# A graph layer on one core: 140 sorted supers in place of 136, and GpSimd's gathers signalled from single products

## The reference

```python
def reference(x, src, dst, edge_type_16, L0_gnn_weight):
    h = jnp.maximum(_layernorm(x, axis=-1), 0.0)
    # _L0_gnn_ref(h, weight, src, dst, etypes):
    h_src = feat[src]
    for r in range(16):
        mask = etypes == r
        msg = msg + h_src * mask[:, None] @ weight[r]
    out = segment_sum(msg, dst, num_segments=6250)
    return x + out
```

## Time and profile before

| | |
|---|---|
| median of three executions | 1234.6 us |
| the profiled execution's own time | 1229.24 us |
| its span | 1227.5 us |
| mean granted clock of TensorE over the span | 0.983 |
| TensorE products (PE) busy | 1081.7 us, 88% |
| VectorE (DVE) busy | 918.1 us, 75% |
| ScalarE (ACT) busy | 437.2 us, 36% |
| GpSimd (POOL) busy | 708.6 us, 58% |
| chain that ended last, by engine | PE 70%, issue 10%, DVE 8%, ACT 5% |

### The profile page before, as it was taken

One profiled execution on the slowest core, in us unless ns is written; L12 is line 12 of the kernel. 1 busy time (PEld: TensorE's weight loads), 2 busy tenths in 40 slices (PEclk: granted clock), 3 DMA queues, 4 the chain that ended last, 5 costly groups with the idle time before them and its releaser, 6 DMA issues.

```text
span 1227.5 us, 38318 instructions
## 1 busy us (share of the span) xinstructions
PE 1081.7 (88%) x15079; PEld 724.9 (59%) x15079; DVE 918.1 (75%) x2711; ACT 437.2 (36%) x1128; POOL 708.6 (58%) x674
## 2 busy tenths in 40 slices
PE   3998998888899889899888989989988898898897
PEld 1445665565666656566565656656665665666665
DVE  7756777887777788787777777777777787777774
ACT  4784232333333333333233333333333332333332
POOL 2214666566656666666665666666666666666630
PEclk9999999999999999999999999999999999999999
DMA  6794222111122212121221112222211221212211
GB/s 171 311 393 169 58 59 60 56 49 48 58 60 59 58 49 58 50 58 58 59 58 50 54 52 58 58 60 58 59 52 46 58 57 58 59 58 58 57 35 56
DMA packets 42263, 93.40 MB, mean 76 GB/s; under 512 B 14923, under 2 KB 14925, under 8 KB 42084
## 3 DMA queue, kind: packets, MB, share of 16 engines
q1 hardware_dynamic: 13490, 40.95, 9.7%
q0 software_dynamic: 20640, 21.18, 8.4%
q10 hardware_dynamic: 7954, 28.79, 6.1%
HBM read 63.29 MB, written 27.59 MB: 74 GB/s over the span
## 4 chain that ended last, share of the span: by engine, by line
PE 70%; issue 10%; DVE 8%; ACT 5%; another core or an unknown queue 4%; DMA 3%; ACTq 0%; DVEq 0%; POOL 0%; SPq 0%; POOLq 0%
PE ps L1268 32%; PE ps L1253 19%; PE ps L1295 6%; DVE u L943 3%; ACT u L599 3%; PE ps L1310 2%; PE ps L1170 2%; DMA table<-u 2%; PE ps L1194 2%; PE ps L1161 2%; DMA w_cat<-weight 1%; DVE spreadv L855 1%; PE ps L1112 1%; PE ps L1183 1%
## 5 line engine op out<-in xcount | busy, mean ns | idle before, releaser
L526 POOL DMA_INDIRECT u<-table,row_idx x611 | 641.4, 1050 | 402.9 <-PE ps L1268 137.9
L1268 PE MATMUL ps<-u 64*64 64x512 bf16 (+1 forms) x7072 | 471.1, 378 | 35.1 <-issue 30.6
L669 ACT CAST u<-ps 128x384 bf16<-128x384 f32 (+1 forms) x612 | 256.4, 465 | 582.5 <-PE ps L1253 492.8
L943 DVE TENSOR_SCALAR u<-iota_key,z_sb 128x512 bf16<-128x512 f16 x1156 | 351.2, 368 | 112.2 <-PE ps L1268 78.1
L1268 PEld LDWEIGHTS ps<-u 64*64 64x64 bf16 x7072 | 213.1, 106 | 231.5 <-issue 110.2
L1253 PE MATMUL ps<-parts,u 128*128 128x192 bf16 x3332 | 328.3, 250 | 23.0 <-issue 21.1
L1253 PEld LDWEIGHTS ps<-parts,u 128*128 128x128 bf16 x3332 | 271.5, 99 | 57.6 <-issue 53.9
L933 DVE TENSOR_SCALAR u<-u,node_id 128x1152 bf16<-128x1152 f16 (+2 forms) x408 | 178.6, 493 | 0.0
L678 ACT COPY u<-ps 128x512 f32<-128x512 f32 x136 | 73.1, 590 | 75.0 <-remote 44.9
L963 DVE TENSOR_TENSOR accT<-accT,ps 128x32 f32 x238 | 44.7, 188 | 59.9 <-DVE accT L963 21.0
L1295 PE MATMUL ps<-u,w_cat 128*64 128x128 f32 x1088 | 78.8, 278 | 6.3 <-issue 4.7
(11 more groups left out here) (131 smaller groups left out, 643.4 us busy)
## 6 DMA issues: line engine op xcount, KB each, us to landing
u<-rel_dram SPq DMA_DIRECT2D x68, 544.0 KB
table<-u ACTq DMA_DIRECT2D x24, 1024.0 KB, 5.3
u<-table,row_idx POOLq DMA_INDIRECT x611
rel_dram<-rel_row SPq DMA_DIRECT2D x68, 4.2 KB
x_sb<-x SPq DMA_DIRECT2D x2, 448.0 KB
out<-h_sb SPq DMA_DIRECT2D x3, 224.0 KB
out<-h_sb ACTq DMA_DIRECT2D x3, 224.0 KB
msg_x<-table,spill_row POOLq DMA_INDIRECT x34
```

The lines of the kernel that those rows point to most:

```text
L526: pool.indirect_dma_start(out=msg_p[:, b, j, :], out_offset=None, in_=table, in_offset=bass.IndirectOffsetOnAxis(ap=row_idx[:, j, m:m + 1] ...
L669: act.copy(msg_s[:, u % MB, 0:width, :].rearrange("p q c -> p (q c)"), ps[gather_bank(u)][:, 0:width * ROW]).then_inc(s_gev, 1)
L943: dve.tensor_scalar(khot[:, v % KR, :], iota_key[:, :], z_sb[:, n % 3, 1, q:q + 1], None, ALU.is_equal).then_inc(s_khot, 1)
L1268: last = pe.matmul(ps[3 + a][half * D:(half + 1) * D, keys], msg_s[rows, u % MB, q % 2, part * D:(part + 1) * D], khot[rows, v % KR, keys] ...
```

## The change

NS becomes 140, so there are 70 pairs in place of 68 and 35 groups of four in place of 34; the windows of gathered edges go from 102 to 98, their tiles from 611 to 583, and all fetches, with those of the edges left over from the sort, from 645 to 618. The end of 12 supers, in place of 8, is prepared inside the loop.

GpSimd no longer waits for a count of one of eight semaphores. There is one semaphore, `s_go`, that TensorE increments once for each fetch. It does so at any of 4495 modelled spots: each product of `gather` that doesn't end a bank, the fourth product of each range in `sum_sorted`, and each product of `weigh` but the last. The planner's numbers for the pieces of the stream are altered a little, and the least distance of two spots is 1.2 in place of 0.7.

```diff
-    NS, SJ, SQ, SK, SW, GR = 136, 7, 17, 3, 32, 4
+    NS, SJ, SQ, SK, SW, GR = 140, 7, 17, 3, 32, 4
...
-        for b in banks_of(n, c):
-            now += 0.082 * SK * min(2, SQ - 2 * b)
-            marks.append((now, "gat", n * GB + b + 1))
+        for q in ranges_of(n, c):
+            for t in range(q * SK, min(q * SK + SK, NT)):
+                now += 0.082
+                if not ends_bank(q, t):
+                    spots.append(now)
...
-    FIRST, LAST, LANDED, LEAST = 0.0, now - 24.0, 5.0, 0.7
+    FIRST, LAST, LANDED, LEAST = 0.0, now - 24.0, 5.0, 1.2
...
-        mark = min((mark for mark in marks if mark[0] >= due), default=marks[-1], key=lambda mark: abs(mark[0] - at))
-        due = mark[0] + LEAST
+        go = min((s for s in range(len(spots)) if spots[s] >= due), key=lambda s: abs(spots[s] - at))
+        due = spots[go] + LEAST
...
+            def wait_for_sign():
+                begun[0] += 1
+                pool.wait_ge(s_go, begun[0])
...
+            def spot(ins):
+                if passed[0] in signs:
+                    ins.then_inc(s_go, 1)
+                passed[0] += 1
...
-                    if q % 2 == 1 or q == SQ - 1:
-                        last.then_inc(s_gat, 1)
+                        if ends_bank(q, t):
+                            last.then_inc(s_gat, 1)
+                        else:
+                            spot(last)
...
-                        sums(q, 1, 1)
+                        spot(sums(q, 1, 1))
...
+                    if r < R - 1:
+                        spot(last)
                     if r == R // 2 - 1:
-                        last.then_inc(s_mid_fl, 1)
```

More of the change, by code:

```diff
@@ L141, in gnn_program @@
     before = lambda m: m * PJ
-    marks, starts, now = [], [], 0.0
+    ends_bank = lambda q, t: t == NT - 1 or q % 2 == 1 and t == q * SK + SK - 1
+    spots, starts, now = [], [], 0.0
     for i, (n, c) in enumerate(STREAM):
@@ L146, in gnn_program @@
         now += 0.1
-        for b in banks_of(n, c):
-            now += 0.082 * SK * min(2, SQ - 2 * b)
-            marks.append((now, "gat", n * GB + b + 1))
+        for q in ranges_of(n, c):
[3 more added lines that the diff above has]
+                    spots.append(now)
+        now += 0.38 * (turned(n, c) is not None) + 0.31 * (spilled(n, c) is not None)
         if i:
             now += 0.14
[L152 to L160, removed]
+            for b in banks_of(*STREAM[i - 1]):
+                for q in range(2 * b, min(2 * b + 2, SQ)):
+                    now += 0.214
+                    spots.append(now)
+                now += 0.214 if 2 * b + 1 < SQ else 0.107
+        now += 0.5 * (c == 0 and n > 0) + 0.22 * (permuted(n, c) is not None) + 0.45 * (ranked(n, c) is not None)
         if n >= 2 and n % 2 == 0 and c == weigh_at:
-            marks += [(now + 0.95, "mid", n // 2), (now + 1.9, "fl", n // 2)]
-            now += 1.9
+            for r in range(R):
+                now += 0.13
+                if r < R - 1:
+                    spots.append(now)
     starts.append(now)
-    FIRST, LAST, LANDED, LEAST = 0.0, now - 24.0, 5.0, 0.7
-    marks.sort()
+    FIRST, LAST, LANDED, LEAST = 0.0, now - 24.0, 5.0, 1.2
     FETCHES = PALL + NGR
-    fetches, tile_time = [], []
+    spilled_fetch, tile_time, go_spots = [], [], []
     due = 0.0
@@ L176, in gnn_program @@
         at = max(at, starts[2 * four + 1]) if spills else at
-        mark = min((mark for mark in marks if mark[0] >= due), default=marks[-1], key=lambda mark: abs(mark[0] - at))
-        due = mark[0] + LEAST
-        fetches.append((mark, four if spills else None))
+        go = min((s for s in range(len(spots)) if spots[s] >= due), key=lambda s: abs(spots[s] - at))
+        due = spots[go] + LEAST
+        go_spots.append(go)
+        spilled_fetch.append(four if spills else None)
         if not spills:
-            tile_time.append(max(at, mark[0]))
+            tile_time.append(max(at, spots[go]))
     place = [min(n for n in range(NPR) if starts[n] >= tile_time[before(m) + len(tiles_of(m)) - 1] + 1.4 + LANDED or n == NPR - 1)
@@ L341, in gnn_program @@
         s_gp = [sem(f"s_gp{k}") for k in range(PRING)]
-        s_hotp, s_sump, s_mid_fl = sem("s_hotp"), sem("s_sump"), sem("s_mid_fl")
+        s_hotp, s_sump, s_go = sem("s_hotp"), sem("s_sump"), sem("s_go")
         s_over = sem("s_over")
@@ L497, in _ @@
             pool.wait_ge(s_tev, PIECES)
[L498 to L504, removed]
+            begun = [0]
+            def wait_for_sign():
+                begun[0] += 1
+                pool.wait_ge(s_go, begun[0])
             def fetch_spilled():
-                w = fetch_at_mark()
+                w = spilled_fetch[begun[0]]
                 b = w % 2
+                wait_for_sign()
                 pool.wait_ge(s_xwin, w + 1)
@@ L522, in _ @@
                 for j in tiles_of(m):
-                    while fetches[0][1] is not None:
+                    while spilled_fetch[begun[0]] is not None:
                         fetch_spilled()
-                    fetch_at_mark()
+                    wait_for_sign()
                     pool.indirect_dma_start(
@@ L529, in _ @@
                     ).then_inc(s_gp[b], 16)
-            while fetches:
+            while begun[0] < FETCHES:
                 fetch_spilled()
@@ L1233, in _ @@
                     sort_ranks(2)
+            signs, passed = set(go_spots), [0]
+            def spot(ins):
+                if passed[0] in signs:
+                    ins.then_inc(s_go, 1)
+                passed[0] += 1
             def gather(n, c):
```

## The result

The changed kernel takes 1201.0 us (median of 4, 1199.11 to 1205.48) against 1235.0 us of the kernel before beside it: ratio 0.9733, 95% interval 0.9713 to 0.9754. The forecast was 1200 us. The time is as forecast.

What follows compares the result with a forecast made beforehand. TensorE's stream was taken as the bound, with 217 us of holes following GpSimd's fetches. +23 us of work and -57 us from the spread gave -34 from 1234.6, rounded to 1200 us; 8-in-10 range 1148 to 1248.

Steps and rivals of the forecast that it cites:

- The work of two more pairs: TensorE's stream: two more pairs and 28 fewer tiles raise work from 908 to 931 us, +23 us, all on the path.
- The signals: TensorE's products: 618 semaphore increments cost nothing, at worst 6 us.
- The spread: GpSimd's fetches: coming more evenly, they cut the loss from holes in TensorE's stream from 217 to 160 us, gaining 57.
- The factor 0.77: Holes in TensorE's stream per fetch: 0.188 us in place of 0.243, applied to the whole loss.
- a tally by the distance of neighbouring fetches: TensorE's lateness per fetch in the trace: mean 0.243 us, crowded 0.455, evenly spaced 0.10.
- The shares of 60, 25 and 15%: Fetches after the change: 60% even (0.10 us of holes), 25% at today's mean (0.24), 15% crowded (0.455).
- The tally's last figure: Fetches with both preceding distances above 1.7 us: 0.02 us of holes each, in 17 cases.
- The first rival: Holes belong to TensorE's own stream and each added pair brings its own: +31 us, 1266 us; chance 0.12.
- The second: POOL is again late for every second fetch, holes go with the number of fetches: +14 us, 1249 us; chance 0.12.
- The third: The spread of fetches works nearly in full, 104 us of loss: -90 us, 1145 us; chance 0.10.
- The fourth: DVE becomes the bound as a faster TensorE asks for one-hots sooner; 945 us of DVE work; folded into the range.
- The rule that speaks against it: Skill text: engine and DMA ports are disjoint, TensorE never waits on them; by it, spreading fetches would bring nothing.

Runs made afterwards that it cites:

- idle_signs: marks140 plus the changed kernel's increments on TensorE's products, for which nobody waits; GpSimd goes by the old marks: 1198.9 us, ratio 0.9728.
- signs136: Changed kernel's signals with the old 136 supers and old least distance 0.7: 1232.5 us, ratio 1.0007 to the kernel before.
- marks140: Kernel before with 140 supers and its old marks for the fetches: 1193.2 us, ratio 0.9689.
- skip28: Kernel before (136 supers, old marks) with 28 of its 611 ordinary fetches left out, all sums kept: 1200.9 us, ratio 0.9744.
- twins: Changed kernel with every second fetch issued right behind the first, without its own signal: 1214.1 us, ratio 0.9860 to the kernel before.
- few: Changed kernel with only about 50 of 618 fetches issued, TensorE's products unchanged: 1059.7 us, ratio 0.8606 to the kernel before.
- hw_queue: few plus 544 plain DMAs of the same size issued by SyncE, on the third chip: 1050.9 us, ratio 0.9979 to the kernel before.
- signs144: Changed kernel with 144 supers, on the third chip: 1083.4 us, ratio 1.0286 to the kernel before.
- marks144: Kernel before with 144 supers and its old marks: 1165.9 us, ratio 0.9468.

## Why the prediction came out right, and where it was wrong

*The work of two more pairs, +23 us: holds.* The shortest durations of sums and gathers are alike in every kernel (2.07 us for 36 sums), and the third chip is in keeping with it: 1053 to 1100 us for 12 supers more, of which 69 would be work and 22 come back.

*The signals, nothing, at worst 6 us: within that.* idle_signs allows 6 us and signs136 nothing; the runs don't tell them apart.

*The spread, 217 to 160 us of loss: the right sum for the wrong reason.* The loss is 165 us. The factor 0.77 was built from a tally by the distance of neighbouring fetches (0.455 us where crowded, 0.10 where even), and I took the correlation for the lever. This step failed, and four runs say so: signs136, with the finer signals alone, gains nothing; marks140, without them, gains at least as much as the change; skip28, with the old signals and 28 fetches fewer, gains 31 us; twins, with a third more fetches back to back, loses 13 to 16 us, where the tally's prices asked for 75. What stands in its place is that 140 supers bring fewer fetches for each microsecond of TensorE's work, 0.71 to 0.66, which I had in the text only as 1.5 us of even distance. The spacing itself is worth what twins shows, about 0.3 us for each of the 51 fetches that twins puts closer than 1.3 us, where the tally has a difference of 0.36.

That the sum came out is luck: I scaled by number and by a factor for the spread, 0.96 x 0.77 = 0.74. The loss fell to 165 / 217 = 0.76, and marks140, without any finer signals, has 133 / 196 = 0.68 of the cost of fetches before. The shares of 60, 25 and 15% had no source either. The planners' own clocks put 155 of 644 distances under 1.25 us before, none at zero, and 89 after, but 91 with the old marks and 140 supers: they too give the wider spacing to the supers. The tally's last figure, 0.02 us with both distances above 1.7, is said to be of 17 cases; the trace has 51.

*The first rival (holes of TensorE's own)* falls with few: 141 us go when the fetches go, on a chip that has the holes. *The second (POOL stays crowded, +14)* had its mark come true and its price not: 43% of the fetches are still back to back, and the kernel got faster. *The third (in full, 1145)* did not happen, though few shows that there was that much to win. *The fourth* is not seen: DVE is at 78%, with 938 us of the 945 that I had given it.

*The rule that speaks against it*, of the Trainium skill, "SBUF — State Buffer", section "SBUF: two separate sides", says that TensorE never waits on a memory port for others. On the first two chips TensorE's stream does have holes from GpSimd's fetches: 2.58 us for 36 sums against 2.09 without. Whether a memory port is their path no run here tells, so the rule is not contradicted in what it says, but it was no guide to the time.

*What stays open* is what in a fetch holds TensorE up, and why not on the third chip. It is not rows or bytes; it grows steeply as fetches get denser. I had supply of TensorE's instructions in mind; no run tries it, and the late signals speak against it, since a product that is only issued late should still signal on time, as it does on the third chip wherever TensorE waits for another engine. Whether it is GpSimd's part of the fetch or its packets could be told by hw_queue on one of the first two chips, which was not run. Each chip was measured in one session of its own, so that "chip" here may stand for something else that differed between them. The changed kernel itself did not run on the third chip. Half way from the kernel before to signs144 lies 1068 us, slower by 1.4%; that is an estimate.

## What to carry to other kernels

Where one engine's stream is held up by another's actions, do not choose the remedy from a correlation inside one trace: leave the actions out, then thin them out, then bunch them; the three together say how much is in their number and how much in their spacing. Look also at when an engine's signals arrive, and not only at its waits: the lag of TensorE's increments told the disturbed runs from the others at once. Look for the steep part of such a cost: here 28 of 645 fetches were worth 31 us while the average said 9. And time a tuned balance on more than one chip before trusting it, since here 8 supers more win 5.3% on one chip (marks144) and cost 2.9% on another (signs144).

## What the hardware showed that I had not expected

The same kernel takes 1233 us on two chips and 1053 on a third, in runs that agree among themselves within 0.7% on each. As far as two kernels with 144 supers show it, marks144 on the second chip (1166 us) and signs144 on the third (1083), the difference lies in TensorE's holes (PEld's waits before sums 43.4 us and 12.4), while the durations are alike (VectorE's key one-hots 367 and 371 ns). On the first two chips an increment by TensorE is recorded a median of 351 to 594 ns after its product's end while GpSimd fetches, and 14 ns after it on the third. A GpSimd memset of 960 floats per partition, 971 ns, lengthens VectorE's 512-column compare from 349 to 511 ns on average, an indirect DMA issue of 1051 ns only to 368.
